# Scale rows spread by TensorE and fc1 of the first chunk interleaved with the dequantization of int8 weights

## The reference

```python
xn = _layernorm(x)
s  = attn(xn, Wq, Wk, Wv, Wo)          # softplus features, running sums over time
# _L0_ffn_ref(xn, ...), G = 128, H = 1024, F = 4096
h  = (xn - mu) * rsqrt(var + EPS) * ln_gamma + ln_beta
w1 = ((fc1_q - 128.0).reshape(8, 128, F)  * fc1_scales[:, None, :]).reshape(H, F)
y  = silu(h @ w1 + fc1_bias)
w2 = ((fc2_q - 128.0).reshape(32, 128, H) * fc2_scales[:, None, :]).reshape(F, H)
g  = _silu(xn + 0.5 * (y @ w2 + fc2_bias))
x  = x + s * g
```

## Time and profile before

| | us |
|---|---|
| median of 3 timed runs | 4114.27 |
| lowest, highest | 4095.98, 4155.9 |
| the profiled execution | 3851.9 |
| its span, slowest core (of 3835.6 to 3850.3) | 3850.3 |
| mean granted TensorE clock, all cores | 0.804 to 0.806 |
| TensorE matmul busy | 2788.3 (72%) |
| TensorE weight load busy | 1972.5 (51%) |
| VectorE busy | 988.1 (26%) |
| ScalarE busy | 444.3 (12%) |

### The profile page before, as it was taken

One profiled execution on the slowest core, in us unless ns is written; L12 is line 12 of the kernel. 1 busy time (PEld: TensorE's weight loads), 2 busy tenths in 40 slices (PEclk: granted clock), 3 DMA queues, 4 the chain that ended last, 5 costly groups with the idle time before them and its releaser, 6 DMA issues.

```text
span 3850.3 us, 40754 instructions; the slowest of 8 cores (3835.6 to 3850.3 us)
## 1 busy us (share of the span) xinstructions
PE 2788.3 (72%) x16928; PEld 1972.5 (51%) x17088; DVE 988.1 (26%) x1406; ACT 444.3 (12%) x817; POOL 214.5 (6%) x136
## 2 busy tenths in 40 slices
PE   1588887776889888891147777887731388888887
PEld 1466655554666666660035555565520265655564
DVE  2722222313221211213521111021125322222221
ACT  0022222110000000000011111111100011111111
POOL 0000000000000000000000000000000122211222
PEclk9988888885766666665578888988865699999998
DMA  8211111132212120104420000000044311111111
GB/s 176 82 45 55 45 55 55 45 82 61 50 39 44 44 44 18 32 12 147 151 68 23 23 23 23 22 1 23 23 134 146 124 45 44 45 44 31 32 38 33
DMA packets 91685, 214.10 MB, mean 56 GB/s; under 512 B 37488, under 2 KB 54128, under 8 KB 85232
## 3 DMA queue, kind: packets, MB, share of 16 engines
q1 hardware_dynamic: 67888, 100.85, 9.1%
q0 software_dynamic: 12096, 60.30, 5.9%
q10 hardware_dynamic: 11520, 50.34, 4.2%
HBM read 135.97 MB, written 58.72 MB: 51 GB/s over the span
## 4 chain that ended last, share of the span: by engine, by line
PE 67%; DVE 12%; DMA 9%; DVEq 5%; issue 3%; another core or an unknown queue 2%; ACT 1%; POOLq 0%; SPq 0%; ACTq 0%; POOL 0%
PE PS L147 18%; PE PS L148 17%; PE PS L146 17%; DVE AR L169 4%; PE PS L960 3%; PE PS L911 3%; DMA AR<-fc1q 2%; DMA AR<-fc2q 2%; PE PS L954 2%; PE PS L951 2%; DVEq L170 1%; PE PS L916 1%; DMA AR<-x_in 1%; PE PS L930 1%
## 5 line engine op out<-in xcount | busy, mean ns | idle before, releaser
L146 PE MATMUL PS<-AR,WA 128*128 128x256 bf16 x3072 | 861.9, 281 | 44.4 <-DVE AR L620 29.6
L147 PE MATMUL PS<-AR,WA 128*128 128x256 bf16 x3072 | 861.7, 280 | 0.0
L148 PE MATMUL PS<-AR,WA 128*128 128x256 bf16 x3072 | 860.5, 280 | 0.0
L147 PE MATMUL PS<-WA,AR 128*128 128x512 bf16 x1536 | 594.2, 387 | 245.3 <-DVE AR L648 196.0
L148 PE MATMUL PS<-WA,AR 128*128 128x512 bf16 x1528 | 589.7, 386 | 0.0
L146 PE MATMUL PS<-WA,AR 128*128 128x512 bf16 x1384 | 534.0, 386 | 1.2 <-DVE AR L648 0.8
L648 DVE TENSOR_TENSOR AR<-YTMP,AR 128x256 bf16<-128x256 f32 x256 | 129.3, 506 | 1181.4 <-ACT AR L761 1181.1
L146 PEld LDWEIGHTS PS<-AR,WA 128*128 128x128 bf16 x3072 | 309.1, 101 | 120.6 <-issue 53.6
L1004 PE MATMUL PS<-ident_s,AR 128*128 128x128 f32 x256 | 65.8, 426 | 408.7 <-DVEq L610 390.6
L146 PEld LDWEIGHTS PS<-WA,AR 128*128 128x128 bf16 x1536 | 152.6, 99 | 399.2 <-issue 252.2
L147 PEld LDWEIGHTS PS<-AR,WA 128*128 128x128 bf16 x3072 | 308.7, 100 | 66.7 <-issue 0.2
(11 more groups left out here) (95 smaller groups left out, 2380.9 us busy)
## 6 DMA issues: line engine op xcount, KB each, us to landing
AR<-x_in SPq DMA_DIRECT2D x24, 1024.0 KB, 7.7
AR<-s ACTq DMA_DIRECT2D x16, 1024.0 KB, 9.6
AR<-fc1q POOLq DMA_DIRECT2D x16, 1024.0 KB, 10.1
AR<-fc2q POOLq DMA_DIRECT2D x32, 512.0 KB, 5.7
AR<-s ACTq DMA_DIRECT2D x32, 512.0 KB, 4.8
qf_sc<-AR SPq DMA_DIRECT2D x8, 1024.0 KB, 3.9
kf_sc<-AR SPq DMA_DIRECT2D x8, 1024.0 KB, 3.9
v_sc<-AR SPq DMA_DIRECT2D x8, 1024.0 KB, 4.9
```

What stands on the lines that cost most here:

```text
L146: tensor.matmul(out, lh, rh, start=start, stop=False)
L147: tensor.matmul(out, lh, rl, start=False, stop=False)
L148: return tensor.matmul(out, ll, rh, start=False, stop=stop)
```

## The change

Scale rows. The loads to 128 partitions and their semaphores `f_dls` are gone. ScalarE loads each scale row in pieces of 512 numbers (2 KB) to partition 0, into three slots `AR[0:1, 0:1536]` that lie in x's buffer, one piece after another as `srow(m)`, m from 0 to 63. TensorE spreads a piece over 128 partitions with a matmul in float32 whose stationary operand is one row of ones (`AR[0:1, 1536:1664]`), two such matmuls for each unit of 1024 columns (`srep_mm`), into banks 4 and 5 or 6 and 7 in turn.

Units. Both weights are dequantized in units `u` of 1024 columns: 0 to 15 are halves of fc1's tiles, 16 to 31 fc2's tiles. VectorE multiplies with PSUM as an operand (counted by `f_dqr`), ScalarE makes the high part (`f_hic`), VectorE subtracts. Units go in pairs on VectorE.

Order. Layer norm and transposes of chunk 0 come ahead of all dequantization. On TensorE, the spreads stand between the matmuls of fc1: during hidden tile 0 two spreads go before each `kt`, and after each later tile one more for fc2's units. fc2 of chunk 0 comes after all of it, since it accumulates in the banks of the spreads. On ScalarE, Silu of tile `u - 16` comes after the copy of unit `u`.

Queues. fc2's first two int8 tiles are loaded without waiting, on semaphores of their own (`f_dl2`), the others when the unit two before is done. SyncE loads x of chunk 1 only after the half's last spread, as the slots lie in x's buffer.

```diff
                     if c >= 1:
                         sync.wait_ge(f_xc[fi], c)
+                    if c == 1:
+                        sync.wait_ge(f_sbc, 64 * (fi + 1))
...
-                            sync.wait_ge(f_deq[1], 24)
+                            sync.wait_ge(f_deq[1], 32)
...
-                        gpsimd.wait_ge(f_deq[fi], kt - 1)
+                        gpsimd.wait_ge(f_deq[fi], 2 * kt - 2)
...
-                    gpsimd.wait_ge(f_deq[fi], 7 + i)
+                    if i >= 2:
+                        gpsimd.wait_ge(f_deq[fi], 15 + i)
...
-                for pr in range(4):
-                    t0, t1 = 2 * pr, 2 * pr + 1
-                    for sl_ in range(2):
-                        vector.wait_ge(f_dld[fi][sl_], 16 * (pr + 1))
-                        vector.wait_ge(f_dls[fi][sl_], 16 * (pr + 1))
-                    sA, sB = ar(F_DEQ[0], 2048), ar(F_DEQ[1], 2048)
-                    vector.scalar_tensor_tensor(
-                        sA, sA, -128.0, ar(F_SREP[0], 2048), ALU.add, ALU.mult)
-                    vector.scalar_tensor_tensor(
-                        sB, sB, -128.0, ar(F_SREP[1], 2048), ALU.add, ALU.mult)
...
+                def dq_unit(u):
+                    if u < 16:
+                        kt, h = u // 2, u % 2
+                        return (ar(F_DEQ[kt % 2] + h * 1024, 1024),
+                                wb(W1AH + kt * 2048 + h * 1024, 1024),
+                                wb(W1AL + kt * 2048 + h * 1024, 1024))
+                    i = u - 16
+                    return (ar(F_IC2[i % 2], 1024),
+                            wb(W2AH + i * 1024, 1024),
+                            wb(W2AL + i * 1024, 1024))
+
...
                     if c == 0:
-                        for pr in range(8):
-                            i0, i1 = 2 * pr, 2 * pr + 1
-                            for sl_ in range(2):
-                                vector.wait_ge(f_dld[fi][sl_], 16 * (5 + pr))
-                                vector.wait_ge(f_dls[fi][sl_], 16 * (5 + pr))
...
+                        vector.memset(AR[0:1, 1536:1664], 1.0)
+                        vector.drain()
+                        vector.engine_nop().then_inc(f_dqr, 1)
+                        for pu in range(16):
+                            us = (2 * pu, 2 * pu + 1)
+                            for u in us:
+                                stg, dh, dl = dq_unit(u)
+                                if u < 16:
+                                    vector.wait_ge(f_dld[fi][(u // 2) % 2],
+                                                   16 * (u // 4 + 1))
+                                else:
+                                    vector.wait_ge(f_dl2[fi][u % 2],
+                                                   16 * ((u - 16) // 2 + 1))
+                                vector.wait_ge(f_sbc, 64 * fi + 2 * u + 2)
+                                vector.scalar_tensor_tensor(
+                                    stg, stg, -128.0,
+                                    PS[:, 2048 + (u % 2) * 1024:
+                                       2048 + (u % 2) * 1024 + 1024],
+                                    ALU.add, ALU.mult).then_inc(f_dqr, 1)
                             vector.drain()
-                            hA = wb(W2AH + i0 * 1024, 1024)
-                            hB = wb(W2AH + i1 * 1024, 1024)
-                            vector.tensor_copy(hA, sA)
-                            vector.tensor_copy(hB, sB)
+                            for u in us:
+                                stg, dh, dl = dq_unit(u)
+                                vector.wait_ge(f_hic, 32 * fi + u + 1)
+                                vector.tensor_sub(dl, stg, dh
+                                                  ).then_inc(f_deq[fi], 1)
                             vector.drain()
-                            vector.tensor_sub(wb(W2AL + i0 * 1024, 1024), sA, hA
-                                              ).then_inc(f_deq[fi], 1)
-                            vector.tensor_sub(wb(W2AL + i1 * 1024, 1024), sB, hB
-                                              ).then_inc(f_deq[fi], 1)
-                            vector.drain()
-                    for ft in range(16):
-                        vector.wait_ge(f_ysh[fi], 16 * c + ft + 1)
-                        vector.tensor_sub(
-                            arb(F_YL + ft * 256, 256),
-                            YTMP[:, (ft % 2) * 256:(ft % 2) * 256 + 256],
-                            arb(F_YH + ft * 256, 256)).then_inc(f_yev[fi], 1)
+                            if pu >= 8:
+                                for ft in (2 * (pu - 8), 2 * (pu - 8) + 1):
+                                    vector.wait_ge(f_ysh[fi], ft + 1)
+                                    vector.tensor_sub(
+                                        arb(F_YL + ft * 256, 256),
+                                        YTMP[:, (ft % 2) * 256:(ft % 2) * 256 + 256],
+                                        arb(F_YH + ft * 256, 256)
+                                    ).then_inc(f_yev[fi], 1)
+                    else:
+                        for ft in range(16):
+                            vector.wait_ge(f_ysh[fi], 16 * c + ft + 1)
+                            vector.tensor_sub(
+                                arb(F_YL + ft * 256, 256),
+                                YTMP[:, (ft % 2) * 256:(ft % 2) * 256 + 256],
+                                arb(F_YH + ft * 256, 256)).then_inc(f_yev[fi], 1)
 
...
-                for ti in range(24):
-                    is1 = ti < 8
-                    if ti >= 2:
-                        scalar.wait_ge(f_deq[fi], ti - 1)
-                    if is1:
-                        scalar.dma_start(
-                            out=ar(F_SREP[ti % 2], 2048),
-                            in_=s1[ti:ti + 1, fi * 2048:(fi + 1) * 2048]
-                            .partition_broadcast(P)
-                        ).then_inc(f_dls[fi][ti % 2], 16)
+
+                def srow(m):
+                    u_, a_ = divmod(m, 2)
+                    if u_ < 16:
+                        kt_, h_ = u_ // 2, u_ % 2
+                        off = fi * 2048 + h_ * 1024 + a_ * 512
+                        src = s1[kt_:kt_ + 1, off:off + 512]
                     else:
-                        kt = fi * 16 + (ti - 8)
-                        if ti == 8:
-                            scalar.wait_ge(f_tr[fi], 4)
-                        scalar.dma_start(
-                            out=ar(F_SR2[ti % 2], 1024),
-                            in_=s2[kt:kt + 1, :].partition_broadcast(P)
-                        ).then_inc(f_dls[fi][ti % 2], 16)
+                        r_ = 16 * fi + (u_ - 16)
+                        src = s2[r_:r_ + 1, a_ * 512:a_ * 512 + 512]
+                    scalar.dma_start(
+                        out=AR[0:1, (m % 3) * 512:(m % 3) * 512 + 512],
+                        in_=src).then_inc(f_dsl[m % 3], 16)
+
+                def silu_ft(c, ft):
+                    yi = 16 * c + ft
+                    scalar.wait_ge(f_ymm[fi], yi + 1)
+                    if ft == 0 and c >= 1:
+                        scalar.wait_ge(f_zmm[fi], 2 * c)
+                    if yi >= 2:
+                        scalar.wait_ge(f_yev[fi], yi - 1)
+                    scalar.activation(
+                        YTMP[:, (ft % 2) * 256:(ft % 2) * 256 + 256],
+                        bk(2 + ft % 2, 0, 256), AF.Silu,
+                        bias=b1_s[:, fi * 16 + ft:fi * 16 + ft + 1])
+                    scalar.drain()
+                    scalar.copy(arb(F_YH + ft * 256, 256),
+                                YTMP[:, (ft % 2) * 256:(ft % 2) * 256 + 256]
+                                ).then_inc(f_ysh[fi], 1)
+                    if fi == 0 and c == NC1 - 1 and ft == 15:
+                        scalar.nop().then_inc(phb[2], 1)
+
+                scalar.wait_ge(f_xc[fi], 1)
+                for m in range(3):
+                    srow(m)
+                for u in range(32):
+                    scalar.wait_ge(f_dqr, 33 * fi + u + 2)
+                    if u < 16:
+                        kt, h = u // 2, u % 2
+                        stg = ar(F_DEQ[kt % 2] + h * 1024, 1024)
+                        dh = wb(W1AH + kt * 2048 + h * 1024, 1024)
+                    else:
+                        i = u - 16
+                        stg = ar(F_IC2[i % 2], 1024)
+                        dh = wb(W2AH + i * 1024, 1024)
+                    scalar.activation(dh, stg, AF.Copy).then_inc(f_hic, 1)
+                    m0 = 3 if u == 0 else 2 * u + 3
+                    for m in range(m0, 2 * u + 5):
+                        if m < 64:
+                            srow(m)
+                    if u >= 16:
+                        silu_ft(0, u - 16)
                 for c in range(NC1):
-                    for ft in range(16):
-                        yi = 16 * c + ft
-                        scalar.wait_ge(f_ymm[fi], yi + 1)
```

(84 more changed lines are left out.)

## The result

The changed kernel is slower by about 1.1%: ratio to the kernel before 1.011, 95% interval 1.007 to 1.015. Its median is 3904.0 us. Some executions run with a lower clock on one die or both; the ratios leave them out, but the three timed runs of before that the forecast stood on (4114.27) were such ones, as were cores 0 to 3 in the run with the layer norm's new place alone; undisturbed, the kernel before takes 3847 to 3891 us.

The account below looks back on a forecast made before the run. The prediction held chunk 0's stage bound by a load, multiply, cast, subtract loop, not matmuls. Its terms summed to 338.9 us per half against 294.4, +44.5, twice +89, on 4114.27: 4203 us, range 4135 to 4290.

Parts of the forecast that it names:

- x lands: Start of each half: x, 1 MB, lands in 10.2 us beside 3 MB instead of 5; bounds 7.7 and 17.1.
- even to odd hops: fc1 dequantization, multiply to multiply within a pair: 6.2 us each, waiting for a scale row issued after the multiply before.
- odd to even hops: fc1 dequantization, multiply to multiply between pairs: 7.0 us each, with the even subtract, three bf16 matmuls and the spread in series.
- fourteen fc2 units: fc2 dequantization: multiply, copy, Silu, fc1 tile and spread in series without overlap; 10.5 us a unit, 147 for fourteen.
- its end, fc2 of chunk 0: End of the stage: last copy and subtract 2.6 us, then all 192 fc2 matmuls of chunk 0, 43.1 us.
- the base: Whole kernel: the +89 us was added to 4114.27, the median of three timed runs, not to the profiled 3851.9.
- a row's landing: fc1 dequantization: a scale row's small load takes 1.9 us to land, with ends 1.8 and 7.3.
- I use one sum twice: Second half's chunk 0 stage, 297.4 us against 294.4 in the first, gets the same +44.5 us; together +89.
- leave the rest of the kernel as it is: Chunks 1 to 7 of each half and both attention stages: no line edited, so unchanged in the sum.
- a clock that holds: Rival on fc2's units: TensorE's clock stays high, 9.2 us a hop on the mean; +48 us, 4162; chance 0.18.
- low clock throughout: Rival: low clock and slow row landing (3.0), fc2 units 12.3 us; +173 us, 4287; chance 0.22.
- cheap spread: Rival: one pass per column at high clock, 0.22 us per 512 columns; 28 us less per half, 4058; chance 0.07.

Follow-up runs that it names:

- an order alone: Kernel before, broadcast loads kept: VectorE takes two hidden tiles' remainders after each fc2 pair, ScalarE issues two scale loads then two Silus; 0.968 of the kernel before.
- its two follow-ups: To the reordered kernel before, added: chunk 0's layer norm after the first fc1 pair, 0.9626; then second half's partial sums and chunk 1's x loaded early, 0.958.

## Why the prediction failed, by its own steps

| step, first half | forecast | measured |
|---|---|---|
| x lands | 10.2 | 6.8 |
| layer norm, transposes | 15.2 | 14.9 |
| first unit | 5.2 | 5.6 |
| even to odd hops | 8 x 6.2 | 8 x 5.2 |
| odd to even hops | 7 x 7.0 | 7 x 7.4 |
| first fc2 unit | 10.8 | 9.7 |
| fourteen fc2 units | 147 | 146.2 |
| last unit | 6.2 | 5.0 |
| its end, fc2 of chunk 0 | 45.7 | 45.9 |
| sum | 338.9 | 327.5 |

The measured column runs from 1762.5, VectorE's first instruction of the half, to 2090.0, chunk 0's first eviction. Right were the direction, the serial chain of the fc2 units, the price of a spread and the end; the odd to even hops were 0.4 too short. Four steps failed.

That the length of an fc2 unit came out to 1% is partly luck. The 10.5 stood between 12.3, a chain of 9.6, and a hop of 10.4 that would be bound by the fc2q load, taken from the 7.85 us of the kernel before. The load bound no unit: the tile lands in 3.3 us here, and the multiplies wait for the spread. The chain alone is 10.4: 3.3 us up to the fc1 tile (1914.68 to 1918.02), 5.0 for the tile and 2.1 for the spread, where 3.7, 4.2 and 1.7 stood. The clock rose later than the forecast took, at the end of the tile and not within it.

First, the base. The sum of differences was added to 4114.27, of which the forecast said that it lay 262 us above the profiled execution "for a reason that the profile does not show". The measured 3904 agrees with 3851.9 plus 52. Had the difference been put on the profiled execution's own time, the forecast would have been 3941, 37 us too high, and the range, moved by the same 262, 3873 to 4028, which holds the 3904. So this step alone put the time outside the range.

Second, a row's landing and what stands before it. The term took 1.9 us and half of ScalarE's copy. The changed kernel's rows show it:

```profile
1802.78 1.06 ACT L785 ACTIVATE WA<-AR 128x1024 bf16<-128x1024 f32 x1 [6.66 <-DVE AR L635]
1802.80 0.62 ACTq L750 DMA_DIRECT2D AR<-s  x2
...
1804.21 2.04 PE L1028 MATMUL PS<-AR 1*128 1x512 f32 x2 [1.15 <-DMA AR<-s]
```

The issue starts 0.02 us after the copy and runs beside it, and the spread starts 1.4 us after the issue; 1.9 + 0.33 + 0.1 + 0.5 was forecast. That is 9 us per half, over eight hops and the last unit. x's landing was 3.4 too long: 3 MB without the broadcasts landed faster than in proportion.

Third, "I use one sum twice". The second half's stage before was 6 us longer than the first's from eviction to eviction (304.4 against 298.3), which is hidden if it is counted from its first scale load, as the forecast did. In the changed kernel both are equal within 3 us. So +25.3 was measured there where +44.5 stood (by medians over the cores +31.0 in the first half and +27.5 in the second).

Fourth, "leave the rest of the kernel as it is". Chunk 1 of the second half gained 5.7 us with no line of its own edited. The forecast itself let the 43 us of fc2 cover the load of chunk 1's x, and did not ask what comes next in VectorE's list, the layer norm of that x. The experiment with x held back shows that chunk 1 follows it.

Of the rivals, the one with a clock that holds (4162, +48) came nearest in size, the span being 50.6 us longer, but not for its reason: the clock in the fc2 units was 0.66. The low clock throughout is refuted by the same 0.66, the cheap spread by the spread issued twice.

The rule of the Trainium skill that the forecast named ("TensorE: Matmul & The Clock Gate", its section on why this matters for kernels: a matmul of 32 rows takes as long as one of 128) agrees with the runs down to one row, as far as they go: three spreads of 512 columns took 5.46 us at the low clock, 1.71 each plus the end, 3.33 ns per column as with 64 rows. A float32 matmul of 32 or 128 rows like these was not run. The fixed cost of about 2.0 us in the Trainium skill, "DMA: Bandwidth & Descriptors", the anatomy of one DMA, is given there for a transfer from GpSimd's queue, a condition that the forecast left out. A row of 2 KB from ScalarE's queue took less, 1.4 us from issue to use.

## What to carry to other kernels

When work is put between the instructions of another loop, write down for one turn of it what each engine does in order, and look for an instruction that a third engine needs and that stands behind a wait; here moving Silu ahead of the copy was worth 3%, more than the change cost. Before changing how data gets there, ask which engine idles in the stage and why: the kernel before had 80 us of matmuls waiting behind 99 us of loads, and an order alone let them overlap (3.2%, with its two follow-ups 4.2%), while the new way of spreading the scales takes the banks that fc2's part of this overlap needs (that other banks would have helped was not tried). Put a forecast difference on the execution that its rows come from, and follow each engine's list past the end of the edited stage.

## What the runs showed of the hardware

- Float32 matmuls from one row cost 3.33 ns per column at a granted clock of 0.50, 1.71 us per 512 columns: with six slots two of them make the whole hop of 3.41 us. Two at a clock of 1.00 took 1.98 us with their end (1912.59).
- In the fc2 units the mean clock was 0.66 with TensorE busy 96 of 146 us, and 0.91 with it busy 72 of 80 us. Inside one unit it was 0.50 for the fc1 tile that followed 3.5 us of idle time and 1.00 for the spread behind it.
- A DMA issue on ScalarE's queue runs beside the activation that was issued just before it (1802.78 and 1802.80).
- fc1q's tiles, 1 MB each, landed in 4.8 us (median) in the changed kernel, without the broadcasts, and in 10.1 in the kernel before, with them; fc2q's, 512 KB, in 3.3 and 5.7. The pace at which the tiles are asked for changed as well, so the broadcasts are not shown to be the whole cause. After, then before:

```profile
AR<-fc1q POOLq DMA_DIRECT2D x16, 1024.0 KB, 4.8
AR<-fc2q POOLq DMA_DIRECT2D x32, 512.0 KB, 3.3
...
AR<-fc2q POOLq DMA_DIRECT2D x32, 512.0 KB, 5.7
```
